# Attention values by products of 128 rows and eight columns a query group, denominators by ScalarE's accumulator, scores over three pairs of banks

## The reference, cut to what matters

```python
y = jnp.einsum('bnd,hde->bhne', x, Wkqv) + bkqv[None, :, None, :]
k = y[..., :Dm]; q = y[..., Dm:2 * Dm]; v = y[..., 2 * Dm:]
A = jnp.einsum('bhnd,bhmd->bhnm', q, k) / jnp.sqrt(jnp.float32(Dm))
A = jnp.where(mask[None, None], A, -jnp.inf)
A = jax.nn.softmax(A, axis=-1)
sa = jnp.einsum('bhnm,bhmd->bnhd', A, v).reshape(Bm, Nm, Dm)
return sa @ Wp + bp
```

## Time and profile before

| | us |
|---|---|
| median of three runs | 2852.96 (2840.04 to 2853.36) |
| the profiled execution | 2851.38 |
| its span, first to last instruction | 2849.3 |
| TensorE busy | 2547.1 (89%) |
| VectorE busy | 2295.0 (81%) |
| ScalarE busy | 1828.5 (64%) |
| GpSimd busy | 1800.8 (63%) |

### The profile page before, as it was taken

One profiled execution on the slowest core, in us unless ns is written; L12 is line 12 of the kernel. 1 busy time (PEld: TensorE's weight loads), 2 busy tenths in 40 slices (PEclk: granted clock), 3 DMA queues, 4 the chain that ended last, 5 costly groups with the idle time before them and its releaser, 6 DMA issues. The chain is left out here.

```text
span 2849.3 us, 85256 instructions
## 1 busy us (share of the span) xinstructions
PE 2547.1 (89%) x35846; PEld 1550.4 (54%) x35846; DVE 2295.0 (81%) x2551; ACT 1828.5 (64%) x3631; POOL 1800.8 (63%) x1733
## 2 busy tenths in 40 slices
PE   7559999998998888788998999999999999999997
PEld 4224444443443433456665666666666766666665
DVE  5235676797688888689995789988999999899994
ACT  3124444444555555367776788888888888788884
POOL 2023002211276676577775789988999999989992
PEclk9779999999999999899998999999999999999999
DMA  8940000000021211102001111211121121111111
GB/s 76 20 16 8 11 11 8 9 8 24 18 51 53 52 47 52 40 7 89 13 28 58 39 33 28 59 38 30 40 64 39 37 62 38 28 30 33 31 27 36
DMA packets 200171, 99.28 MB, mean 35 GB/s; under 512 B 126147, under 2 KB 196783, under 8 KB 198255
## 3 DMA queue, kind: packets, MB, share of 16 engines
q1 hardware_dynamic: 199791, 93.82, 18.9%
HBM read 67.69 MB, written 7.21 MB: 26 GB/s over the span
## 5 line engine op out<-in xcount | busy, mean ns | idle before, releaser
L818 ACT ACTIVATE prob<-ps,mneg,shift 128x1024 f32<-128x1024 f32 (+7 forms) x384 | 366.3, 954 | 474.3 <-DVE mneg L726 468.8
L605 PE MATMUL ps<-xnT,qp 128*128 128x512 f32 (+3 forms) x1280 | 579.1, 569 | 83.3 <-ACT prob L818 80.8
L726 DVE TENSOR_REDUCE mneg<-ps 128x1 f32<-128x1024 f32 (+7 forms) x384 | 342.9, 893 | 284.6 <-PE ps L609 243.1
L1904 DVE TENSOR_TENSOR area<-ps,tab 128x2048 f32<-128x2048 f32 x192 | 430.6, 2283 | 68.7 <-ACT area L1684 40.1
L605 PEld LDWEIGHTS ps<-xnT,qp 128*128 128x128 f32 x1280 | 220.2, 194 | 360.6 <-issue 201.1
L1415 PE MATMUL ps<-wqk,area 128*128 128x512 f32 x768 | 361.6, 614 | 28.4 <-DVE area L1970 21.4
L2091 POOL TENSOR_TENSOR area<-area,rn 128x1024 f32<-128x1024 f32 x192 | 369.8, 1947 | 7.5
L1505 PEld LDWEIGHTS ps<-wvo,area 128*128 128x128 f32 x3072 | 353.7, 193 | 26.9 <-issue 20.9
L1505 PE MATMUL ps<-wvo,area 128*128 128x128 f32 x3072 | 360.4, 276 | 3.3 <-ACT area L1733 3.3
L734 DVE STREAM_TRANSPOSE area<-prob 128x1024 f32<-128x1024 f32 (+7 forms) x384 | 353.8, 922 | 8.3 <-ACT prob L818 6.5
L679 PE MATMUL ps<-area,vb 32*32 32x256 f32 (+7 forms) x12288 | 298.6, 333 | 67.0 <-POOL vb L946 43.6
(11 more groups left out here) (272 smaller groups left out, 4394.0 us busy)
## 6 DMA issues: line engine op xcount, KB each, us to landing
xe<-bc_scratch SPq DMA_DIRECT2D x128, 128.0 KB, 3.0
area<-bc_scratch SPq DMA_DIRECT2D x128, 128.0 KB, 4.1
staged<-values_scratch SPq DMA_DIRECT2D x192, 36.0 KB, 1.9
wqk<-lwqk_dram SPq DMA_DIRECT2D x6, 1024.0 KB, 6.4
xp<-xc SPq DMA_DIRECT2D x96, 48.0 KB, 2.7
xc<-xs SPq DMA_DIRECT2D x96, 32.0 KB
wvT<-lwvT_dram SPq DMA_DIRECT2D x6, 512.0 KB, 7.9
wo<-lwo_dram SPq DMA_DIRECT2D x6, 512.0 KB, 9.4
```

The source lines that it names most:

```text
L605: mm = E.matmul(ps[:, r + o // 512, 0:w], k.qp[:, group % 2, i * P:(i + 1) * P], k.xnT[:, k0 + o:k0 + o + w], start=True, stop=not (o + w ...
L726: V.tensor_reduce(k.mneg[:, U:U + 1], ps[:, r:r + 2, :].rearrange("p a b -> p (a b)")[:, 0:nk], X_AXIS, ALU.max, negate=True).then_inc(s(" ...
L818: A.activation(k.prob[:, U % 2, 0:nk], ps[:, r:r + 2, :].rearrange("p a b -> p (a b)")[:, 0:nk], ACT.Exp, bias=k.mneg[:, U:U + 1], scale=k ...
L1904: V.tensor_tensor(k.rot[:, n % 2, w, :, :].rearrange("p c (h d) -> p c h d", d=DH), bcast(heads(what, n), 1, 2), bcast(k.tab[:, n % FRAME, ...
```

## The change

- Value columns are stored without the ones (8 instead of 9), head by head, and saved by three DMAs in place of 32.
- `vb` holds, for each block of keys, 32 columns: eight for each row group, zero in the others. GpSimd makes it by a product with `own`, in place of the copy. Then one product of 128 rows and 32 columns does what four of 32x32 did. They run in pieces 1 to 7 of the next batch.
- Values of batch b go to bank 6 + b % 2, and are copied out, gathered (32 products of 128x32 by eight columns) and copied on for each batch by itself.
- exp gives its sum in `dsum` by its accumulator output.
- In the first half the mask is added in PSUM by VectorE, ahead of the maximum; in the second half its product comes ahead of the scores.
- Scores use three pairs of banks, 0 to 5, and are issued three slots ahead.
- The first visits and the steps that feed them are a step later; the last reciprocal moves ahead of the stage's end.

```diff
@@ opening_sp, opening_pool, opening_dve @@
+    S.dma_start(k.own[:], d["own"]).then_inc(s("rest"), 16)
...
-    G.memset(k.valL[:, :, :, DV0], 1.0)
-    G.memset(k.vb[:], 0.0).then_inc(s("g"), k.g.up())
...
-            ins = V.tensor_tensor(k.valL[:, i, :, 0:DV0], ps[...]
+            ins = V.tensor_tensor(k.valL[:, :, i, :], ps[...]
@@ constants of the stage @@
-VB = 2 * VW + WIN
 STRIDE = (KB, KB - P)
+PAIRS = 3
...
-VISITS = {7: ("sa", 0), 9: ("out", 0), 17: ("hat", 0),
+VISITS = {8: ("sa", 0), 10: ("out", 0), 17: ("hat", 0),
...
-    return (5, 5, 5, 5, 6, 6) if is_square(b) else (2, 4, 5, 6, 7, 8)
+    return (4, 4, 4, 5, 5, 5, 5) if is_square(b) else (2, 3, 4, 5, 5, 6, 7)
...
-    if b == 0 or not 1 <= i <= 6:
+    if b == 0 or i == 0:
@@ attention_sp @@
-        for h in heads:
-            S.dma_start(k.v_d[h, half].rearrange("c a n -> (c a) n"), k.valL[:, tiles, h, :]).then_inc(s("vd"), 16)
+        S.dma_start(k.v_d[heads, half].rearrange("h c a n -> (c a) h n"), k.valL[:, heads, tiles, :].rearrange("p h t v -> p h (t v)")).then_inc(s("vd"), 16)
...
-    save_values(range(2), 0)
-    S.wait_ge(s("vd"), 32)
+    save_values(slice(0, 2), 0)
+    S.wait_ge(s("vd"), 16)
     stage_values(0)
     stage_values(1)
-    save_values(range(2, H0), 0)
+    save_values(slice(2, H0), 0)
...
-                S.wait_ge(s("vd"), 16 * H0)
-                save_values(range(H0), 1)
+                S.wait_ge(s("vd"), 32)
+                save_values(slice(0, H0), 1)
@@ attention_pe: scores @@
-        group, r = group_of(b), 2 * (z % 2)
+        group, r = group_of(b), 2 * (z % PAIRS)
...
-        diag = not is_square(b)
+        masked = (nk - P) // 512 if BATCH[b][2] else None
+        if masked is not None:
+            o = (nk - P) % 512
+            E.matmul(ps[:, r + masked, o:o + P], k.identb[:], k.causal[:], start=True, stop=False, skip_group_check=True)
...
-        if diag:
-            j, o = (nk - P) // 512, (nk - P) % 512
-            mm = E.matmul(ps[:, r + j, o:o + P], k.identb[:], k.causal[:], start=False, stop=True, skip_group_check=True)
@@ attention_pe: values, gather, the loop @@
-            if j == 0 and turn:
-                E.wait_ge(s("oL"), turn)
+            if b >= 2:
+                E.wait_ge(s("oL"), b - 1)
...
-            for q in range(4):
-                at = slice(WIN * q, WIN * (q + 1))
...
-                mm = E.matmul(ps[WIN * c:WIN * (c + 1), 4 + q, WIN * i0:WIN * NTH], k.vb[at, x, NTH * c + f // 4, VB - WIN - VW * j:VB - VW * j], of,
+            mm = E.matmul(ps[WIN * c:WIN * (c + 1), 6 + x, WIN * i0:WIN * NTH], k.vb[:, x, NTH * c + f // 4, :], of, start=f < 4, stop=f >= HALF - 4,
...
-        E.wait_ge(s("ot"), turn + 1)
+        E.wait_ge(s("ot"), b + 1)
         for i in range(NTH):
-            mm = E.matmul(ps[:, 4, 256 + 3 * VW * i:256 + 3 * VW * (i + 1)], k.oT[:, i, :, :].rearrange("p q n -> p (q n)"), k.pick[:], start=True, stop=True,
+            for q in range(4):
+                mm = E.matmul(ps[WIN * q:WIN * (q + 1), 6 + b % 2, 256 + DV0 * i:256 + DV0 * (i + 1)], k.oT[:, b % 2, WIN * i:WIN * (i + 1)],
+                              k.pick[:, DV0 * q:DV0 * (q + 1)], start=True, stop=True, skip_group_check=True)
...
-        if z + 2 < len(SLOTS):
+        if z + PAIRS < len(SLOTS):
             pair_free(z)
-            issue(z + 2)
-        if what == "piece" and U % NTH == NTH - 1 and U // NTH - 1 in LAST_OF:
-            gather(LAST_OF[U // NTH - 1])
+            issue(z + PAIRS)
+        if what == "piece" and U % NTH == 1 and U // NTH >= 2:
+            gather(U // NTH - 2)
+    gather(NB - 2)
     values(NB - 1, range(HALF))
-    gather(len(TURNS) - 1)
+    gather(NB - 1)
@@ attention_dve @@
+        if U < FIRST:
+            V.tensor_tensor(of[:, nk - P:nk], of[:, nk - P:nk], k.causal32[:], ALU.add).then_inc(s("v"), k.v.up())
+            V.wait_ge(s("v"), k.v.n)
+        V.tensor_reduce(k.mneg[:, U:U + 1], of, X_AXIS, ALU.max, negate=True).then_inc(s("top"), 1)
...
-            V.wait_ge(s("oL"), FIRST_TURNS)
-            V.reciprocal(k.rec0, k.oL1[:, :, :, DV0]).then_inc(s("half_dve"), ev.up("rec"))
-        elif j == 6:
+            V.reciprocal(k.rec0, k.dsum[:, 0:FIRST].rearrange("p (h i) -> p h i", i=NTH)).then_inc(s("half_dve"), ev.up("rec"))
+        elif j == 7:
@@ attention_act @@
-                     bias=k.mneg[:, U:U + 1], scale=k.unit[:, g, h:h + 1]).then_inc(s("prob"), 1)
+                     bias=k.mneg[:, U:U + 1], scale=k.unit[:, g, h:h + 1], accum_out=k.dsum[:, U:U + 1]).then_inc(s("prob"), 1)
...
-        A.activation(k.oT.rearrange("p i q n -> p q i n"), ps[:, 4:8, 0:WIN * NTH].rearrange("p q (i n) -> p q i n", n=WIN), ACT.Copy).then_inc(s("ot"), 1)
+        A.activation(k.oT[:, b % 2, :], ps[:, 6 + b % 2, 0:WIN * NTH], ACT.Copy).then_inc(s("ot"), 1)
...
-        if i == NTH - 1 and b - 1 in LAST_OF:
-            values_out(LAST_OF[b - 1])
-        elif i == 0 and b - 2 in LAST_OF:
-            gathered(LAST_OF[b - 2])
+        if i == 0 and b >= 2:
+            values_out(b - 2)
+        elif i == 2 and b >= 2:
+            gathered(b - 2)
@@ attention_pool @@
-        G.tensor_copy(k.vb[:, b % 2, :, 2 * VW:3 * VW], k.staged[:, b % 2, :, :].rearrange("p c (t v) -> p (c t) v", v=VW)).then_inc(s("vb"), 1)
+        G.tensor_tensor(k.vb[:, b % 2, :, :].rearrange("p f (q v) -> p f q v", q=4), bcast(k.staged[:, b % 2, :, :].rearrange("p c (t v) -> p (c t) v", v=DV0), 2, 4),
+                        bcast(bcast(k.own[:], 1, HALF), 3, DV0), ALU.mult).then_inc(s("vb"), 1)
...
+        G.tensor_tensor(total, total, w, ALU.mult)
...
+        G.tensor_tensor(totals[:, :, 0, :], totals[:, :, 0, :], totals[:, :, 1, :], ALU.add)
```

More of the change, by code:

```diff
@@ L605, in scores @@
             mm = E.matmul(ps[:, r + o // 512, 0:w], k.qp[:, group % 2, i * P:(i + 1) * P], k.xnT[:, k0 + o:k0 + o + w],
-                          start=True, stop=not (o + w == nk and diag), skip_group_check=True)
-        if diag:
-            j, o = (nk - P) // 512, (nk - P) % 512
-            mm = E.matmul(ps[:, r + j, o:o + P], k.identb[:], k.causal[:], start=False, stop=True, skip_group_check=True)
+                          start=o // 512 != masked, stop=True, skip_group_check=True)
         mm.then_inc(s("score"), 1)
@@ L661, in values @@
     def values(b, steps):
-        x, j, turn = b % 2, PLACE[b], TURN_OF[b]
+        x = b % 2
         if not steps:
@@ L812, in exp @@
         b, i, k0, nk = piece(U)
-        r, (h, half, part) = 2 * (z % 2), BATCH[b]
+        r, (h, half, part) = 2 * (z % PAIRS), BATCH[b]
         g = NTH * half + i
@@ L1044, in branch @@
             elif j == J + 2:
-                combine(n + 1, h0, h1, TURN_OF[H0 + 2 * h1 - 1] + 1)
+                combine(n + 1, h0, h1, H0 + 2 * h1)
     def outputs(u):
@@ L1071, in attention_pool @@
     output("mo", 1)
-    combine(len(COMBINE) + 1, COMBINE_LAST, H0 - 1, TURN_OF[NB - 3] + 1)
-    combine(len(COMBINE) + 1, H0 - 1, H0, len(TURNS))
+    combine(len(COMBINE) + 1, COMBINE_LAST, H0 - 1, NB - 2)
+    combine(len(COMBINE) + 1, H0 - 1, H0, NB)
 TURNED = NT // 4
@@ L2213, in build @@
         k.wp, k.rec0 = sb("wp", [P, P])[:], sb("rec0", [P, H0, NTH])[:]
[L2214 removed]
+        k.v_d = nc.dram_tensor("values_scratch", [H0, 2, 4, WIN, NTH * DV0], F32).ap()
         with ExitStack() as c:
@@ L2218, in build @@
             here = Area(area)
-            k.valL = here.take(P, NT, H0, VW)
-            k.oL1 = here.take(P, H0, NTH, VW)
+            k.valL = here.take(P, H0, NT, DV0)
+            k.oL1 = here.take(P, H0, NTH, DV0)
             here = Area(area)
             k.y0, k.delta = here.take(P, ET, TH), here.take(P, ET, TH)
-            k.oL2, k.work = here.take(P, 2 * H0, NTH, VW), here.take(P, ET, TH)
+            k.oL2, k.work = here.take(P, 2 * H0, NTH, DV0), here.take(P, ET, TH)
             k.probT = [here.take(P, NTH * KB), here.take(P, NTH * STRIDE[1] + P)]
@@ L2333, in constants @@
             turn[o + (f + DH // 2) % DH, o + f] = sign[f] * np.sin(phi[f]) * fac[f]
-    c["pick"] = np.tile(np.eye(32, 3 * VW, dtype=np.float32), (4, 1))
+    c["pick"] = np.tile(np.eye(WIN, dtype=np.float32), (4, 1))
+    c["own"] = np.repeat(np.eye(4, dtype=np.float32), WIN, axis=0)
     c["turn"] = turn.astype(np.float32)
```

97 lines of the change are left out of this document (49 added, 48 removed).

## The result

| | before | after |
|---|---|---|
| median, us | 2851.45 (2840.04 to 2853.36, 4 runs) | 2707.18 (2704.77 to 2713.59, 4 runs) |
| profiled execution, its span | 2851.38, 2849.3 | 2704.77, 2703.0 |

The direction and most mechanisms held; the size did not.

What follows compares the result with a forecast made beforehand. Bounds: a DMA stall (batches 0 to 3), TensorE (4 to 15, nearly 16 to 31), VectorE and GpSimd around scans (32 to 47). -80.9 + 2.5 - 16 - 11 + 27 - 3 = -81.4, so 2851.4 becomes 2770 us, range 2736 to 2818.

Steps and rivals of the forecast that it cites:

- The stall: Batches 0 to 3: saving values in fewer, longer packets ends GpSimd's wait for `staged`, -80.9 us.
- Third pair: Score banks: TensorE's waits for exp shrink, 0.15 us a batch in batches 4 to 15, 9 us in 16 to 31.
- Value products: TensorE, each batch: 64 products of 128x32 replace 256 of 32x32, -0.8 us a triangular batch, similar for a square one.
- Gather: TensorE, each batch: 64 instructions of 128x32 by 8 columns, +0.35 us a batch, bounds 0.6 + 0.16 and 1.8 us.
- Mask: First 16 batches: taking the mask's products off TensorE saves 0.5 us a batch.
- Adds in batch 0: VectorE's mask adds count in full in batch 0, +2.5 us, and are hidden from batch 1 on.
- The product on GpSimd: Filling `vb` holds up VectorE's scans in batches 32 to 47, 1.7 us each, +27 us; 5 us in batches 16 to 31.
- The rival that the hold doesn't happen: GpSimd's product does not delay VectorE's scans, -27 and -5 us: 2738 us, chance 0.17.
- the one of exposed weight loads: Full-height weight loads on TensorE are not hidden, 1.7 us a batch in 27 batches, +45: 2815 us, chance 0.14.
- the last rival: TensorE's column groups don't run side by side at full height, so batches stream four times as long: about 3063 us, chance 0.03.
- Accumulator: ScalarE: exp's accumulator output costs 0 to 0.3 us a piece and is hidden.
- End of the stage: The last batch's values, running alone, take 5 to 6 us instead of some 8: -3 us (-5 to +2).

Runs made afterwards that it cites:

- the repeat: The changed kernel, unedited, run again on the chip of the experiments: 2701.01 us, ratio 0.9545 against the kernel before.

## Why the prediction was wrong in size

**The stall: right.** Forecast -80.9, measured -79.4 by the save alone in the profiles, 71 by the medians on one chip. Four batches at TensorE's pace and the packet count were enough; the 62 ns a packet, taken as the pessimistic price, did no harm.

**Third pair: the step that failed.** I gave it 0.15 us a batch in batches 4 to 15 and "about a third, 9 us" of the idle time of batches 16 to 31, about 11 us; no row stood behind either share. Without it the kernel is 47 us slower in the profiles, 43 or 55 by the ratios. I sized it from the idle time of the kernel before, 5.0 and 25.1 us, and added it to the other terms as if they were apart. They are not. In batches 4 to 15 it is worth 7.6 us with TensorE's mask, and 15.7 with the adds. I had the adds hidden because VectorE has time to spare, but with two pairs they lengthen a wait of TensorE (idle 6.2 to 12.9 us), and the third pair is what hides them. In batches 16 to 31 it is the shorter products, with the product on GpSimd: the values' busy time fell by 1.47 us a batch, 23.6 us in all, of which only 10.3 came through with two pairs, while TensorE's idle time rose from 25.1 to 39.1 us. Waits for exp are part of that rise (19.6 us before, 26.1 with two pairs); the rest I have not taken apart. The clock behind the gaps adds 10 us to the 16 of idle time there. The idle time of the old trace was therefore no bound for this term.

**Value products: mechanism right, term small.** Triangular -1.09 a batch (4.83 to 3.74) for -0.8; over batches 16 to 31, half of them square, -1.47 a batch by busy time (103.41 us, then 79.84). A triangular one has -1.01 by that measure (5.25 to 4.24), which leaves an estimated -1.9 for a square one, where I had "a similar gain" to the 0.8. **Gather:** about 0 for +0.35: its 64 instructions take 0.55 us from start to next start (0.73 busy, 0.6 before), 8.6 ns each, at the lower of my bounds (the 9 ns of the stretch of 64). The upper one was worked out wrongly: a quarter of the 128-column load's 194 ns is 49 ns, not 27. **Mask:** 0.31 us of TensorE a batch for 0.5. **Adds in batch 0:** 2.6 us over batches 0 to 3 for 2.5, but by luck: I had all of it in batch 0, and moving that batch's masks alone brought 0.8 there and 0.4 in all. In batches 4 to 15 the adds are hidden, but only because of the third pair.

**The product on GpSimd: right in kind, slightly large.** The hold is +1.3 (square) and +1.55 (triangular), 22.1 us by the run without it, for 1.7 each and 27; it also costs batches 16 to 31 some 7 us by an estimate (2.8 measured, plus 16 x 0.26 of dearer loads) for my 5. That the stretch grew by 17.3 and not by 22 is 4.8 us between the kernel before and the one without the product (385.8 to 381.0). I had counted nothing there; TensorE's shorter work is the likely source, but no run takes it apart.

The rival that the hold doesn't happen is out. So is the one of exposed weight loads: the eight value instructions of 224 columns and their loads take 0.51 us (212.16 to 212.67) where the old form's took 0.59 for 256 columns; exposed loads would have added 1.7 us a batch. The Trainium skill ("TensorE: Matmul & The Clock Gate", Part 3, The mechanism) has a bullet by which a load overlaps products in flight only where its row group differs, while the text above it also lets one go ahead that targets the background weight buffer. These loads all use the same 128 rows and are hidden, so the trace disagrees with the bullet, which the prediction named, and not with the text. The column groups run side by side, which ends the last rival: four key blocks take no longer than two. The Trainium skill ("GPSIMD Engine Reference", 8. Key points) says that GpSimd shares its SBUF interfaces with VectorE and contends with its instructions in a two-port performance mode or with two SBUF inputs. The scans' 1.39 to 2.94 us agree, and instructions of one input did not grow: the transpositions of 128 and 256 columns, which the product meets in every batch from 4 to 15, take 300 and 434 ns there, and as much in the kernel without the product.

**Accumulator:** hidden, as forecast. **End of the stage:** -5.5 for -3. The last values and gather in the trace:

```profile
1048.04 3.32 PE L668 MATMUL ps<-area,vb 128*32 128x256 f32 x64
1051.87 0.72 PE L678 MATMUL ps<-pick,ys 128*32 128x8 f32 x64 [0.52 <-ACT ys L836]
```

3.32 us where I had 5 to 6.

**After the stage: a term that I had not.** Windows of all that follows it, before and after, and after again:

```profile
1191.80:2849.30 1657.50, 1523.07 (x21348) 1054.28 (x21348) 1473.27 (x1434) 1300.90 (x2938) 1388.38 (x1344) 0.98 0.16 39
```

```profile
1055.00:2703.00 1648.00, 1515.02 (x21348) 1053.67 (x21348) 1472.91 (x1433) 1301.96 (x2938) 1389.61 (x1344) 0.98 0.17 40
```

```profile
1053.40:2697.80 1644.40, 1513.36 (x21348) 1050.65 (x21348) 1471.90 (x1433) 1300.71 (x2938) 1388.33 (x1344) 0.99 0.16 40
```

TensorE's same 21,348 instructions are 8 to 10 us shorter and VectorE, ScalarE and GpSimd the same to 1.5 us, so it is TensorE's clock; from 209 to 509 us after the stage's end the granted clock was 0.94 before and 0.97 after. But over the other eight profiles in the table the rest takes 1644 to 1654 us, without following how fast the stage is, and the repeat's 1644.4 lies below both ranges that I had expected for it. I count it as a scatter of some 10 us to which the profiled execution of before was the slow end; whether the shorter stage has a part in it stays open.

Of the 65 us between forecast and profile, 36 are the third pair's (47 less 11), 10 lie after the stage, 10 in the overpriced stretch with scans, and the other 9 are small terms of value products, gather and the end.

## What to carry to other kernels

Idle time in the old trace is no upper bound for what a deeper buffer brings, if the same change shortens the work that covered a wait or puts an instruction into its chain: lay out the timeline with the new work first, then ask which wait is bare, and count the clock behind the gap with it. "Its engine has time to spare" hides an added instruction only if no one waits for its result. A two-input instruction on GpSimd was paid for by VectorE's two-input scans beside it. A strided DMA destination did the same spreading copy for the price of dearer weight loads (3.1 us in batches 4 to 15), and gave 22 us in batches 32 to 47 and some 20 in the whole stage.

## What the runs showed of the hardware that I had not expected

Float32 products of 128x32 tiles on two to four column groups, of 224 to 256 columns, cost 0.51 to 0.56 us for four to eight instructions with the switch of shape, and 8.6 ns an instruction at eight columns, with their loads hidden. Weight columns 32 B apart in place of packed raise the busy time of such a load from 29 to 37 ns by the windows (22.02 and 28.27 us for 768), and the values by 0.26 us a batch. The accumulator's read is an instruction of its own on ScalarE behind every exp; its row is 0.197 us long, but leaving it out freed only 0.09 us of ScalarE a piece.
